# Linear attention: the tensor step sorted into two fp32 and two fp32r stretches, other engines' orders to match, and a scale chain without its factor of a quarter

## What is computed

```python
q = hidden_states @ Wq; k = hidden_states @ Wk; v = hidden_states @ Wv
beta = jax.nn.sigmoid(hidden_states @ Wb + bb)
gate = silu(hidden_states @ Wg)
q = silu(causal_dwconv(q, qconv_w, qconv_b))     # four taps
k = silu(causal_dwconv(k, kconv_w, kconv_b))
q = layernorm(q.reshape(Bs, Ls, H, DK), qn_w, qn_b)   # (x - m) * rsqrt(var + eps) * w + b
k = layernorm(k.reshape(Bs, Ls, H, DK), kn_w, kn_b)
def step(S, inp):
    S = (1.0 - b) * S + b * (v_t[..., :, None] * k_t[..., None, :])
    o_t = jnp.einsum('bhvk,bhk->bhv', S, q_t)
o = o * gate
return o @ Wo
```

## Time and profile before

| | |
|---|---|
| median of 3 runs | 1284.45 us (1283.82 to 1286.77) |
| the profiled execution, its time | 1285.09 us |
| its span, first to last instruction | 1283.3 us |
| TensorE / VectorE / ScalarE / GpSimd busy | 92% / 76% / 59% / 44% of the span |
| linear attention | about 389 to 1225 us of the span |

### The profile page before, as it was taken

One profiled execution on the slowest core, in us unless ns is written; L12 is line 12 of the kernel. 1 busy time (PEld: TensorE's weight loads), 2 busy tenths in 40 slices (PEclk: granted clock), 3 DMA queues, 4 the chain that ended last, 5 costly groups with the idle time before them and its releaser, 6 DMA issues. The chain is left out here.

```text
span 1283.3 us, 22653 instructions
## 1 busy us (share of the span) xinstructions
PE 1177.3 (92%) x7062; PEld 913.7 (71%) x7062; DVE 971.3 (76%) x2038; ACT 756.1 (59%) x1400; POOL 569.5 (44%) x1066
## 2 busy tenths in 40 slices
PE   4799999996887899999999999999999999999778
PEld 3343434335645798898998988898889899898656
DVE  6767777755435888888888898888798888889552
ACT  2156565673434666676767667666667576666423
POOL 5000000000702566666667667567566666666520
PEclk9599999999887999999999999999999999999989
DMA  4212222201102011111011010200110101010020
GB/s 150 68 45 51 52 48 59 46 7 46 69 4 97 26 39 58 39 30 65 25 36 58 36 37 14 80 25 25 69 37 25 69 25 37 25 37 13 1 66 1
DMA packets 26605, 55.77 MB, mean 43 GB/s; under 512 B 5367, under 2 KB 10359, under 8 KB 25399
## 3 DMA queue, kind: packets, MB, share of 16 engines
q1 hardware_dynamic: 26551, 55.11, 14.0%
HBM read 39.95 MB, written 2.29 MB: 33 GB/s over the span
## 5 line engine op out<-in xcount | busy, mean ns | idle before, releaser
L555 DVE TENSOR_REDUCE a_neg_max<-a_scores 128x1 f32<-128x512 f32 x236 | 154.9, 684 | 64.3 <-PE a_scores L359 64.0
L1519 DVE SCALAR_TENSOR_TENSOR l_conv<-l_proj_q,par,l_conv 128x511 f32<-128x511 f32 (+2 forms) x192 | 142.4, 742 | 54.9 <-ACT l_conv L1431 51.3
L497 ACT ACTIVATE a_probs<-a_scores_t 128x1024 f32<-128x1024 f32 x128 | 124.2, 1022 | 58.5 <-PE a_scores_t L374 57.6
L1437 ACT ACTIVATE l_conv<-l_conv,par 128x512 f32<-128x512 f32 x128 | 92.3, 722 | 97.7 <-DVE l_conv L1519 97.4
L1519 DVE SCALAR_TENSOR_TENSOR l_conv<-l_proj_k,par,l_conv 128x511 f32<-128x511 f32 (+2 forms) x192 | 142.8, 744 | 7.4 <-DVE l_conv L1519 0.8
L1528 DVE TENSOR_TENSOR_SCAN l_decay<-l_keep,l_diag 128x256 f32<-128x256 f32 (+1 forms) x256 | 147.9, 639 | 0.0
L1241 POOL TENSOR_TENSOR l_k_tok<-l_normed,k_norm 128x256 f32<-128x256 f32 x64 | 56.4, 881 | 167.1 <-ACT l_normed L1448 167.1
L86 POOL MEMSET ln_minus_half_b<- 128x4 f32 x1 | 0.1, 101 | 281.0 <-POOLq L611 281.0
L359 PE MATMUL a_scores<-a_k_stack,a_q_stack 48*128 48x512 f32 x236 | 108.2, 503 | 15.8 <-DVE a_neg_max L555 12.5
L359 PEld LDWEIGHTS a_scores<-a_k_stack,a_q_stack 48*128 48x128 f32 x236 | 42.3, 191 | 106.1 <-DVE a_neg_max L555 87.6
L1448 ACT ACTIVATE l_normed<-l_turn_q,l_shift,l_scale 128x128 f32<-128x128 f32 x256 | 96.2, 456 | 19.9 <-POOL l_shift L1233 19.4
(11 more groups left out here) (292 smaller groups left out, 3432.1 us busy)
## 6 DMA issues: line engine op xcount, KB each, us to landing
l_keep<-keep_rows SPq DMA_DIRECT2D x64, 384.0 KB, 3.5
head_raw<-w_heads SPq DMA_DIRECT2D x8, 1024.0 KB, 4.8
a_q_stack<-a_dense_hi SPq DMA_DIRECT2D x64, 64.0 KB, 2.2
a_k_stack<-a_dense_hi SPq DMA_DIRECT2D x64, 64.0 KB, 2.2
x_tok<-x SPq DMA_DIRECT2D x4, 512.0 KB, 6.4
a_q_stack<-a_dense_lo SPq DMA_DIRECT2D x32, 64.0 KB, 2.2
a_k_stack<-a_dense_lo SPq DMA_DIRECT2D x32, 64.0 KB, 2.2
wo_raw<-w_o SPq DMA_DIRECT2D x1, 2048.0 KB, 10.8
```

What stands on the lines that cost most here:

```text
L497: act.activation(probs[:, n % 2, 2 * half:2 * half + 2, :], scores_t[half][:], ACT.Exp, scale=SOFT_SCALE).then_inc(probs_done, 1)
L555: dve.tensor_reduce(neg_max[:, g % 2, at:at + 1], max_bank(g, j), AX.X, ALU.max, negate=True).then_inc(max_done, 1)
L1437: act.activation(conv[:, w, m, :], conv[:, w, m, :], ACT.Silu, bias=par[:, h, 2 * TAPS + w:2 * TAPS + w + 1]).then_inc(act_sem[w], 1)
L1519: ins = dve.scalar_tensor_tensor(conv[:, w, m, s:], proj[w][:, 0:SEQ - s], par[:, h, tap:tap + 1], conv[:, w, m, s:], ALU.mult, ALU.add)
```

## The change

It does three things, all in the linear attention.

1. TensorE's step is put in another order: both turns back, both projections (q, k), both turns of tokens, scores and read-out, then the gate's projection, the output projection, and the values' projection last. Fp32 and fp32r products so form two stretches each in a step.
2. ScalarE's and VectorE's steps follow. ScalarE: `gated_high` after both taps, `silu` of q ahead of the gate, the state copy between the two `normalise`, `silu` of k last. VectorE: the gating ahead of the last convolution step of k, the scan ahead of the values, the addition at the step's end and one step sooner for its unit (u - 5 instead of u - 6).
3. In `scales` the product with a tile of quarters is dropped: the sum is made of four times the variance, so scale and shift come out halved, and the gains of q and k are doubled once at the start of the stage.

```diff
             pool.memset(minus_half[:], -0.5).then_inc(consts_set, 1)
-            pool.memset(quarter[:], 0.25).then_inc(consts_set, 1)
+            gains = norm[:].rearrange("p (w c) -> p w c", c=2)[:, :, 0]
+            pool.tensor_scalar(gains, gains, 2.0, 0.0, ALU.mult, ALU.add).then_inc(consts_set, 1)
+            pool.tensor_scalar(k_norm[:, 0, :], k_norm[:, 0, :], 2.0, 0.0, ALU.mult, ALU.add).then_inc(consts_set, 1)
...
-                wait(pool, stat_step, 4 * v + 1)
+                wait(pool, stat_step, 3 * v + 1)
                 pool.tensor_tensor(small[:, 3, :], small[:, 1, :], small[:, 1, :], ALU.mult)
-                pool.tensor_scalar(small[:, 4, :], small[:, 2, :], 1.0 / DK, EPS, ALU.mult, ALU.add).then_inc(stat_step, 1)
-                wait(pool, stat_step, 4 * v + 2)
-                pool.tensor_tensor(small[:, 6, :], small[:, 3, :], quarter[:], ALU.mult).then_inc(stat_step, 1)
+                pool.tensor_scalar(small[:, 4, :], small[:, 2, :], 4.0 / DK, 4 * EPS, ALU.mult, ALU.add).then_inc(stat_step, 1)
+                wait(pool, stat_step, 3 * v + 2)
+                pool.tensor_tensor(small[:, 7, :], small[:, 3, :], small[:, 4, :], ALU.add).then_inc(stat_step, 1)
                 pool.tensor_scalar(small[:, 5, :], small[:, 0, :], -0.5, 0.0, ALU.mult, ALU.add)
-                wait(pool, stat_step, 4 * v + 3)
-                pool.tensor_tensor(small[:, 7, :], small[:, 6, :], small[:, 4, :], ALU.add).then_inc(stat_step, 1)
-                wait(pool, stat_step, 4 * v + 4)
+                wait(pool, stat_step, 3 * v + 3)
                 pool.tensor_tensor(scale[:, i, :], small[:, 7, :], minus_half[:], ALU.pow).then_inc(scales_ready, 1)
...
             def step(pair, k, u):
-                for w in range(2):
-                    if has(u, 2):
+                if has(u, 2):
+                    for w in range(2):
                         turn_back(u - 2, w)
-                    if has(u, 0):
+                if has(u, 0):
+                    for w in range(2):
                         if k == 0:
                             wait(pe, w_ready, 4 * (pair - 1) + w + 1)
                         wait(pe, conv_sem[w], u)
...
-                if has(u, 0):
-                    if k == 0:
-                        wait(pe, w_ready, 4 * (pair - 1) + G + 1)
-                    wait(pe, values_done, u)
-                    project(proj_gv, G, k).then_inc(g_proj, 1)
...
                 if has(u, 0):
                     if k == 0:
-                        wait(pe, w_ready, 4 * (pair - 1) + V + 1)
-                    wait(pe, gate_act, u + 1)
-                    project_values(k).then_inc(v_proj, 1)
+                        wait(pe, w_ready, 4 * (pair - 1) + G + 1)
+                    wait(pe, values_done, u)
+                    project(proj_gv, G, k).then_inc(g_proj, 1)
...
+                if has(u, 0):
+                    if k == 0:
+                        wait(pe, w_ready, 4 * (pair - 1) + V + 1)
+                    wait(pe, gate_act, u + 1)
+                    project_values(k).then_inc(v_proj, 1)
...
                 if has(u, 0):
+                    silu(pair, k, u, 0)
                     wait(act, g_proj, u + 1)
                     wait(act, gated_done, u - 3)
                     act.activation(gate[:, k % 4, :], proj_gv[:], ACT.Silu).then_inc(gate_act, 1)
-                    silu(pair, k, u, 0)
-                    silu(pair, k, u, 1)
                 if has(u, 1):
                     normalise(*before, 0)
-                    normalise(*before, 1)
                 if has(u, 2):
...
                     act.activation(state[:, k % 2, :], score_b[:, 2 * P:2 * P + DK], ACT.Copy).then_inc(state_done, 1)
+                if has(u, 1):
+                    normalise(*before, 1)
+                if has(u, 0):
+                    silu(pair, k, u, 1)
```

More of the change, by code:

```diff
@@ L1109, in linear_attention @@
         minus_half = sb("minus_half", [P, 2 * TPB])
-        quarter = sb("quarter", [P, 2 * TPB])
         diag = sb("diag", [P, SEQ])
@@ L1273, in gated_low @@
                                    ALU.subtract).then_inc(gated_lo_done, 1)
-            pool.wait_ge(consts_set, 4)
+            pool.wait_ge(consts_set, 5)
             def step(pair, k, u):
@@ L1476, in step @@
                     norm_affine(u - 2, (k - 2) % BODY, 0)
-                if has(u, 4):
-                    gated_high(u - 4, (k - 4) % BODY)
                 if has(u, 0):
@@ L1484, in step @@
                     tap(pair, k, u, 1)
+                if has(u, 4):
+                    gated_high(u - 4, (k - 4) % BODY)
                 if new_weights:
@@ L1532, in step @@
             def step(pair, k, u):
-                if has(u, 6):
-                    v, kk = u - 6, (k - 6) % BODY
-                    n = (kk // 2) * TPB + 2 * (kk % 2)
-                    wait(dve, out_done, v + 1)
-                    wait(dve, added, v - 2)
-                    dve.tensor_tensor(x_tok[:, n:n + 2, :], outp[:].rearrange("p (t d) -> p t d", t=2),
-                                      x_tok[:, n:n + 2, :], ALU.add).then_inc(added, 1)
                 if has(u, 0):
@@ L1554, in step @@
                     convolve(pair, k, u, 1, 2)
+                if has(u, 3):
+                    v, r = u - 3, (k - 3) % 4
+                    wait(dve, read_out, v + 1)
+                    wait(dve, gate_act, v + 1)
+                    wait(dve, gated_lo_done, v - 1)
+                    dve.tensor_tensor(gated[:, r % 2, :], outp[:], gate[:, r, :], ALU.mult).then_inc(gated_done, 1)
+                if has(u, 0):
                     convolve(pair, k, u, 1, 3)
@@ L1563, in step @@
                     mask(score_b, v, k, SEQ, CAUSAL - SEQ).then_inc(masked_b, 1)
-                if has(u, 3):
-                    v, r = u - 3, (k - 3) % 4
-                    wait(dve, read_out, v + 1)
-                    wait(dve, gate_act, v + 1)
-                    wait(dve, gated_lo_done, v - 1)
-                    dve.tensor_tensor(gated[:, r % 2, :], outp[:], gate[:, r, :], ALU.mult).then_inc(gated_done, 1)
+                if has(u, 1):
+                    v, kk = u - 1, (k - 1) % BODY
+                    wait(dve, keep_loaded[kk % 4], keep_count(pair, k, 1))
+                    wait(dve, masked_b, v)
+                    wait(dve, k_decayed, v)
+                    scan(kk % 4, range(TPB)).then_inc(decay_done, 1)
                 if has(u, 0):
@@ L1579, in step @@
                         ALU.mult).then_inc(values_done, 1)
-                if has(u, 1):
-                    v, kk = u - 1, (k - 1) % BODY
-                    wait(dve, keep_loaded[kk % 4], keep_count(pair, k, 1))
-                    wait(dve, masked_b, v)
-                    wait(dve, k_decayed, v)
-                    scan(kk % 4, range(TPB)).then_inc(decay_done, 1)
-            dve.wait_ge(consts_set, 4)
-            steps(dve, step, 7, last_apart=True)
+                if has(u, 5):
+                    v, kk = u - 5, (k - 5) % BODY
+                    n = (kk // 2) * TPB + 2 * (kk % 2)
+                    wait(dve, out_done, v + 1)
+                    wait(dve, added, v - 2)
+                    dve.tensor_tensor(x_tok[:, n:n + 2, :], outp[:].rearrange("p (t d) -> p t d", t=2),
+                                      x_tok[:, n:n + 2, :], ALU.add).then_inc(added, 1)
+            dve.wait_ge(consts_set, 5)
+            steps(dve, step, 6, last_apart=True)
 def build(nc, x, w_qkv, w_proj, b_proj, w_in, w_mid, w_out, w_beta, b_beta, w_heads, w_o, params, norms, k_norms, out):
```

## The result

The changed kernel takes 1309.71 us in the median of 4 runs (1306.38 to 1312.36), against 1284.13 us for the kernel before in 4 runs beside it (1282.47 to 1286.77). The ratio is 1.0196, with a 95% interval of 1.0165 to 1.0227: slower by 2.0%. The forecast was 1309 us.

The account below looks back on a forecast made before the run. TensorE's own work, 12.25 us a unit, was taken to bound the kernel; a 12.93 us loop adds 18.5 us over seven pairs and 6 in the first: 1285.1 + 24.5 = 1309.6, median 1309 us. Range 1290 to 1328.

Parts of the forecast that it names:

- What bounds the kernel before: Linear attention: TensorE never waits inside a pair, each unit costs its own work, 12.25 us; 3.3 us more at a pair's start.
- Step 1, seams: TensorE's changes between fp32 and fp32r products: halving them gains at most 0.6 us in all; taken as 0.
- Step 2, the loop: TensorE's k-turn waits on ScalarE's normalise k, behind gate and gate projection: 12.93 us a unit against 12.23 of work.
- Step 3, the side ways: Two other ways into the same loop, through GpSimd's scales and VectorE's masks before the state copy; neither was to bind.
- (a): Way through k's statistics and GpSimd's scales to normalise q: 9.43 us after the k-turn starts, just under the gate's 9.66.
- (b): Way through VectorE's gating, convolution and masks to the state copy: done at 10.4 us, due at 11.03, cover 0.6.
- Step 4, the scale chain: GpSimd's scales without the quarter: 0.4 us saved, worth nothing in the kernel before; in the changed one, without it, loop 13.1.
- Step 5, the pair's start: TensorE's waits of 1.18 and 1.04 us on low halves leave; GpSimd's holding up of scales costs about 0.5, between 0 and 1.2.
- The signs: Units 12.8 to 13.1 us, one k-turn wait of 0.6 to 0.7, no low-half wait before gate projection, TensorE under 96% busy.
- The normalising keeps its spacing: Rival: ScalarE's normalising pieces start 0.39 us apart instead of 0.345, loop 13.3, 1331 us; chance 0.05.
- late masks: Rival: VectorE's masks end over 0.6 us late and hold the state copy; 0.3 beyond gives 13.2, 1326 us; chance 0.13.
- The side of the gain: Rival: the loop is shorter than TensorE's work, units 12.24 us, a pair 98.0 + 0.5, 1267 us; chance 0.09 for faster.

Follow-up runs that it names:

- more_seams: Kernel before, with the gate's six products laid between the score products (16 type changes a unit instead of 8): 1282.67 us, ratio 0.9994.
- k_turn_back: Changed kernel, with the turn of k put back between the projections of q and k: 1275.58 us, ratio 0.9954 to the kernel before.
- state_last: Changed kernel, with ScalarE's state copy put back behind both normalising groups: 1301.26 us, ratio 1.0142 to the kernel before.
- early_k_turn_in_before: Kernel before, with only the turn of k moved ahead of both projections: 1326.47 us, ratio 1.0324.
- old_scale_in_after: Changed kernel, with the product with the quarter back in the scales and gains not doubled: 1326.80 us, ratio 1.0344 to the kernel before.
- gate_before_readout: Changed kernel, with TensorE's gate projection moved ahead of the read-out: 1333.64 us, ratio 1.0384 to the kernel before.

## Why the prediction was right

- **What bounds the kernel before.** Right. Units of 12.25 us were TensorE's work: they stay at 12.23 to 12.28 in five more kernels that differ in seams, order, weights and scales.
- **Step 1, seams.** Right: 0 taken, and neither eight seams more (more_seams) nor two fewer (k_turn_back) make a unit longer or shorter by more than 0.03 us.
- **Step 2, the loop.** Right in its place and its sum: 12.93 predicted, 12.87 measured. Term by term in the unit above: to the gate's start 772.61 - 763.33 = 9.28 (9.19, and the 0.09 for the restart, nearly all of which sits here: the spacing behind the waiting turn is longer); gate to normalising 0.49 (0.47); to the state 1.37 (1.37); copy 0.16 (0.16); normalising of k 1.54 (1.51). The one term that was off is the hand-over from ScalarE to TensorE: 0.05 us, taken as 0.14. The rows it came from the earlier trace rows are those of another hand-over, from the copy of k (one instruction of 512 columns) to a turn of tokens. That one is 0.14 to 0.15 us wherever it occurs in these traces, and the one behind the normalising (its last piece has 128 columns) is 0.05 or 0.06. The trace of the kernel before has the right one too, once the units thin out at the end of the stage; its two rows stand below the list. With the move undone, the loop vanishes (k_turn_back); 0.16 taken out of it comes off the unit (state_last); the early turn alone makes a loop of the same kind, through the scales (early_k_turn_in_before). This is shown, not argued.
- **Step 3, the side ways.** (a) was to be 0.23 short of binding. 0.21 lie between the shift and the normalising, and a normalising that waits for the shift starts 0.03 behind it (old_scale_in_after), so it was 0.18. (b) was to have 0.6 of cover; it had 0.83: the masks end 10.31 us after the turn of k for 10.4, and the copy comes at 11.14 for 11.03. Neither binds inside a pair.
- **Step 4, the scale chain.** In the changed kernel right: 0.60 us measured from L1225 to L1230, and without it a unit of 13.10 where 13.1 was said. For the kernel before it was wrong: "worth nothing" overlooked that GpSimd's queue ends in the values' low half, on which TensorE waits at the pair's start, and that ScalarE's queue carries the gain on to the copy of k. It is worth 4.5 us there. This did not enter the forecast's sum, but the same oversight is in step 5.
- **Step 5, the pair's start.** Half right. The gate's wait left. The values' wait did not leave (0.6 of 1.04 stays), though the step took both to be long ready: it did not add up GpSimd's queue in the new step. The fence below shows it for the first step of the pair above: from the late rows of q at 700.47 to the end of the values' low half at 709.65 GpSimd has 9.2 us of work with no gap over 0.2, and TensorE comes to the values 0.6 us too soon. Against a steady unit the pair's first one is 1.4 us longer, 0.9 at the values and 0.5 at the output product; the next one gives 0.3 back, as its turn of k finds the normalising done, and the third 0.1. So the start costs 1.0 us and not 0.5; within its bounds of 0 to 1.2.
- **Sum.** The loop is 0.06 shorter (8 x 0.06 = 0.5 us less in a pair), the start 0.5 dearer: they cancel, 103.96 for 103.9. Seven pairs at +2.65 are 18.6 (18.5 predicted), the first pair +5.2 (+6 predicted), the rest, at both ends, +2.3 (0 predicted). So 24.5 was forecast and 26.1 measured between the profiled executions, 25.6 between the medians. That the forecast is good to 1 us is partly luck.
- **The signs.** Units of 12.87 us, a wait at the turn of k released by the normalising, and none on a low half before the gate came as said. Two did not come as said. TensorE's busy share in a pair is 96.7% (100.52 of 104.00), where under 96% was named: the records next to a wait are counted longer. And the wait reads 0.39 us by its row and 0.54 by the spacing, not 0.6 to 0.7; the rest of the 0.64 between 12.87 and 12.23 is the slower restart behind it.
- **The rivals.** The normalising keeps its spacing: 1.37 for four pieces. The trace does not agree with the estimate of 387 ns from piece to piece, from the Trainium skill, "ScalarE: Activation LUTs" (section "What ACT_TABLE_LOAD costs"): it shows 342 ns. The masks are in time; what late masks alone would cost was not tried, as gate_before_readout has another wait on its path. The side of the gain was right in its kind: once the loop is under TensorE's work, the pairs' starts decide, as in k_turn_back, 0.5% faster than before. Its price of 1267 us was 9 us too low: it put a pair at 98.5, and in k_turn_back a pair is 100.17, since a start still costs 2.0 us.

The hand-over from the normalising to the turn of k in the kernel before (1203.37 + 1.52 = 1204.89 to 1204.94), for step 2:

```profile
1203.37 1.52 ACT L1448 ACTIVATE l_normed<-l_turn_k,l_shift,l_scale 128x128 f32<-128x128 f32 x4
1204.94 0.66 PE L1337 MATMUL l_turn_k<-ident,l_normed 128*128 128x128 f32 x4 [0.74 <-ACT l_normed L1448]
```

GpSimd's timeline of the changed kernel at that pair's start, for step 5:

```profile
700.47 0.73 POOL L1245 TENSOR_TENSOR l_q_late<-l_qk,l_keep 128x256 f32<-128x256 f32 x1 [1.52 <-ACT l_qk L1463]
...
702.65 1.27 POOL L1265 TENSOR_TENSOR head_lo<-head_raw,head_hi 128x512 fp32r<-128x512 f32 x1
703.88 1.27 POOL L1271 TENSOR_TENSOR l_gated_lo<-l_gated,l_gated_hi 128x512 fp32r<-128x512 f32 x1
...
708.37 1.28 POOL L1265 TENSOR_TENSOR head_lo<-head_raw,head_hi 128x512 fp32r<-128x512 f32 x1
```

## What to carry to other kernels

In a software pipeline over in-order engines, the order inside a step can close a loop of two engines that is longer than any engine's work. Busy shares don't show it (here 91% and 57%); adding spacing of starts along the hand-overs, round to the same instruction of the next step, does, here to within 0.1 us, from the trace before the change. Take each hand-over from a row of the same two instructions. Move first what a waiting instruction needs late, and test a reordering by taking each move back alone: one matmul group of 0.44 us, moved, made the difference between 2.0% slower and 0.5% faster. And an edit on an engine that is idle for a third of the time can be worth something wherever its queue ends in something that the bound engine waits for, even once in eight units.

## What was not expected of the hardware

- How long a matmul starts behind the activation that it waits for depends on the pair of instructions, and hardly varies otherwise: 0.05 us behind the four pieces of 128 columns of the normalising (776.17 to 776.22), 0.14 behind the copy of 512 columns (792.24 to 792.38). What of the two instructions makes the difference was not tried.
- A restart costs beyond the wait: the four turns of k read 0.66 us instead of 0.60, and the gate's start, 9.28 us behind the turn, comes 0.09 later than the spacings of an unbroken flow add up to.
- Changing between fp32 and fp32r products from one instruction to the next has no price that shows: units of 12.233 us with the products interleaved and 12.25 without.
